# First attention layer: reciprocal rows repeated through DRAM and multiplied by GpSimd, output projection at the fourteenth head, one addition for the values' bias, three key stores

## Chip, cores and metric

One core of one Trainium2 chip runs the whole program. The metric is the device time of one execution in microseconds (us). The program is 13,733 instructions on five engines: TensorE (PE, with its weight loads as PEld), VectorE (DVE), ScalarE (ACT), GpSimd (POOL) and the SyncE queue (SP) that issues nearly all DMAs.

## What is computed

Two blocks of cross attention and mixture of experts over x of shape 16 x 128 x 256 (16 batches). Only the first attention is touched. For one batch, with 16 heads of 8 channels, T = 256 positions:

```python
q = Wq @ layernorm(x) + bq;  k = Wk @ ctx + bk;  v = Wv @ ctx + bv      # (128, T)
scores = einsum('hkt,hks->hts', q, k) / sqrt(8)
out = einsum('hts,hks->hkt', softmax(scores), v).reshape(128, T)
x = x + tanh(g_xattn[0]) * (Wo @ out + bo)
```

Then follow a sparse layer of 32 experts (routing, gathers, expert products), a second attention of 8 heads whose keys are the context itself, and a second sparse layer.

## The kernel before

The first attention is a software pipeline over steps t = -5 to 18. In step t, TensorE works through the 16 heads k of batch t (scores a second time as ST, for the exponential, and the product with the values) and through the scores S of the heads that lie 28 heads ahead, whose maxima VectorE takes. Each engine has one program, written out by hand in order, and waits on semaphores: a stalled instruction holds everything behind it on that engine. The same holds for SyncE's issues.

Per head: `scores` issues two S matmuls and two ST matmuls; there are two S banks, so the S of a head waits until VectorE has reduced the head two before it (L432). ACT exponentiates pairs of heads (L353). `values` (O, L478) runs behind heads 2, 3, 6, 7, 10, 11, 14, 15.

One PSUM bank, M1, is passed round the small products of a step; `bank()` waits until the last user's reader is done. In the order of step t: `projections` of batch t+4 behind head 1 (L503, L505), `maxima` of t+1 behind head 5 (L513), `context` (the values of t+1) behind head 9 (L494), `denominators` of t-2 behind head 12 (L520), `output` of t-2 behind head 15 (L527).

The softmax division is done late. The values' product carries a row of denominators for each head. In step b+1 SyncE copies these rows from OS into `dn` (L240) and the numerators into `on` (L243). VectorE takes `reciprocals` in step b+2 behind head 0 (L628), SyncE moves them to `rT` (16 rows, L207), TensorE spreads the rows over 128 partitions with a matmul by a 0/1 matrix (`denominators`, L520), VectorE multiplies `on` with that (`normalized`, L634, behind head 13), and TensorE multiplies by Wo (L527). ACT adds the bias and gates (`rd`, L363, first thing in step b+3, ahead of the first exponential), GpSimd adds to X (L284, first in its step b+3).

GpSimd's step t is, in order: X add (L284), the root for the layer norm (L288, waits for VectorE's statistics, taken behind head 0), the normed row (L292), four instructions that split q and k into bf16 parts (L299, L316, L319, L325), four that split the context's keys for the second attention (L269 to L275), and then `meanwhile(t)`: in step 14 the roots of the next layer's norm for rows 0 to 7 (two L788), in step 15 for rows 8 to 11 (L788).

SyncE's step t is, in order: context load (L162), the spreads of q and k parts (L174, six), the reciprocals' DMA between them (L207), dn (L240), on (L243), the shifted row (L212), a weight load or two, six key stores (L182).

VectorE adds the values' bias in two instructions behind head 10 (L669). The step's other VectorE work in steps 14 and 15 belongs to the next layer: normed rows (L1222) of rows 0 to 3 behind head 11 and of 4 to 7 behind head 15 of step 14, of 8 to 11 behind head 6 of step 15; TensorE transposes them (L833) behind heads 2, 5, 9 and 13 of step 15, each one only after the copy of the one before (L1242, behind heads 4, 6, 10, 14).

Of the kernel before, what the change touches and what calls it, by code (L numbers as in the profile page):

```python
# [15 lines left out]
P = 128  # L16
# [43 lines left out]
class Layer:  # L60


    def __init__(self, name, H, R, sem, before=None, gathers=None, keys=None, kept=None):
# [58 lines left out]


# [53 lines left out]
def keys_stored(e, w, A, M, b):  # L177

    w.wait_ge(A.keys, 4 * (b + 1))
    rows = M["keys_d"][b].rearrange("(i k) (g t) -> i g k t", k=8, g=8)  # L180
    for k in range(6):
        e.dma_start(rows[:, :, k, :], M["KW"][b % 2][:, TERMS[k][1], :]).then_inc(A.kept[b % 2], 16)  # L182


def keys_loaded(e, A, M, b):

    lo = 2048 * A.stack(b) + 1024
    e.dma_start(M["QSall"][:, lo:lo + 1024], M["keys_d"][b]).then_inc(A.ldc[b % U], 16)


def attention_sp(e, w, A, M, loads, behind_first=None):
# [4 lines left out]
    for t in A.steps():  # L196
# [7 lines left out]
        def reciprocals():  # L204
            w.wait_ge(A.rr, b5 + 1)
            w.wait_ge(A.rb, b5 - 1)
            e.dma_start(M["rT"][b5 % 2][0:H, :], M["rdn"][:, 0:2 * H]).then_inc(A.rT, 16)  # L207

# [8 lines left out]
        if within(b1):  # L217
            if not A.first and b1 >= U:

                w.wait_ge(A.st, A.NP * (b1 - U + 1))  # L220
                keys_loaded(e, A, M, b1)
            w.wait_ge(A.res2, b1 + 1)
            w.wait_ge(A.st, A.NP * (b1 - U + 1))
            for k in range(3 if b1 == 0 else 6):
                spread(e, A, M, b1, k)
                if k == 2 and within(b5) and A.first:
                    reciprocals()
            if b1 == 0 and behind_first:
                behind_first()
        elif within(b5) and not A.late(b5):  # L230
            reciprocals()
# [5 lines left out]
        if within(b4):  # L237
            w.wait_ge(A.oe, (NQ // 2) * (b4 + 1))
            w.wait_ge(A.rr, b4)
            e.dma_start(M["dn"][:, 0:2 * H], M["OS"][1:98:32, 0:NQ, :]).then_inc(A.den, 16)  # L240
            on = M["on" + A.name]
            w.wait_ge(A.pm, b4 - len(on) + 1)
            e.dma_start(on[b4 % len(on)][:, :], M["OS"][0:P:NQ, 0:NQ, :]).then_inc(A.num, 16)  # L243
        if within(b2):
# [14 lines left out]
def attention_pool(e, w, A, M, meanwhile=lambda t: None):  # L259
    H = A.H  # L260

    def keys(b):
# [4 lines left out]
        w.wait_ge(A.kept[b % 2], 96 * (b // 2))  # L267
# [9 lines left out]
    for t in A.steps():  # L277
# [135 lines left out]
def attention_pe(e, w, A, M, meanwhile=lambda t, k: None):  # L413
# [155 lines left out]
def attention_dve(e, w, A, M, meanwhile=lambda t, k: None):  # L569
# [60 lines left out]
    def normalized(b):  # L630
        on = M["on" + A.name][b % len(M["on" + A.name])]
        w.wait_ge(A.num, 16 * (A.n0 + b + 1))
        w.wait_ge(A.rb, b + 1)
# [76 lines left out]
class Routed:  # L710


    def __init__(self, sem):
# [19 lines left out]
        self.again0 = [96 * NB // 2, 96 * NB // 2, 32, 0, 0]  # L733
# [9 lines left out]
def ffn0_sp(e, w, G, A, B, M, d):  # L743
# [14 lines left out]
    def stack_ready(b):  # L758

        for k in range(2):  # L760
            w.wait_ge(B.kept[k], 96 * NB // 2)
# [1310 lines left out]
def allocate(nc, ctx, d):  # L2072
# [12 lines left out]
    for nm, shape, dt in (("VA", [P, 2, 16, 32], F32), ("QKc", [P, 2, T], F32), ("QKs", [P, 3, 2, T], BF16),  # L2085
                          ("st6", [P, 6], F32), ("mv", [P, 2], F32), ("ve", [P, 1], F32), ("rs", [P, 1], F32),
                          ("mx", [P, 2, 16], F32), ("mxT", [16, T], BF16), ("rT", [16, T], F32), ("on", [P, T], F32)):
        M[nm] = [sb(f"{nm}{n}", shape, dt) for n in range(2)]
    Cbs = sb("Cb", [P, U, T])
# [82 lines left out]
    M["keys_d"] = nc.dram_tensor("keys", [NB, P, 4 * T], F32, kind="Internal").ap()  # L2172
# [40 lines left out]
def build(nc, d, out):  # L2213
    with ExitStack() as ctx:
# [9 lines left out]
        hole, filled, gates, gamma = (sem(nm) for nm in ("hole", "filled", "gates", "gamma"))  # L2224
# [79 lines left out]
        def act_program(e):  # L2304
# [6 lines left out]
            e.activation(M["tg"][:, :], M["graw"][:, 0:4], ACT.Tanh).then_inc(gates, 1)  # L2311
# [25 lines left out]
        def dve_program(e):  # L2337
# [8 lines left out]
            def gated(t, k):  # L2346
                if t == -3 and k == 1:
                    w.wait_ge(gates, 1)
# [19 lines left out]
def orders():  # L2368
# [9 lines left out]
    return cx, cq, cv, cw  # L2378


def layout(inp):
    a = {k: np.asarray(v) for k, v in inp.items()}
    cx, cq, cv, cw = orders()
# [3 lines left out]
    for n in "qkv":  # L2387
        d["W" + n] = a["L0_xattn_W" + n][cv if n == "v" else cq][:, cx].T
# [3 lines left out]
    d["bv"] = a["L0_xattn_bv"][cv].reshape(1, 128)  # L2392
# [49 lines left out]
```

## Time and profile before

| what | value |
|---|---|
| median of 3 runs | 733.22 us (731.4 to 738.88) |
| the profiled execution | 734.11 us, span 732.3 us |
| TensorE busy | 652.4 us, 89% of the span |
| VectorE busy | 517.6 us, 71% |
| ScalarE busy | 370.8 us, 51% |
| GpSimd busy | 355.1 us, 48% |
| DMA moved | 101.12 MB, mean 138 GB/s |

The span is that of one execution's instructions; the time has about 1.8 us around it. The rows quoted below are from this execution, and their times are counted from the start of its span. The first attention lies between 19 us and 263 us.

### The profile page before, as it was taken

The numbers are of one execution on the slowest core, as the hardware profiler recorded it, in microseconds if no ns is written. First come the engines' busy times: TensorE is split into PE (matmuls) and PEld (weight loads), VectorE is DVE, ScalarE is ACT, GpSimd is POOL, SyncE is SP. The second block draws the span as 40 slices with busy tenths as digits, with TensorE's granted clock in tenths as the row PEclk, the third lists the DMA queues.
The fourth block names the chain that finished last, engine by engine and source line by source line (L and its number), as shares of the span: only waits on it lengthen the run. The fifth ranks groups of instructions, "written<-read, shape, count | busy, mean of one in ns | idle before, by whom it ended". The sixth has DMA issues, their size and how long they took to land.

```text
span 732.3 us, 13733 instructions
## 1 busy us (share of the span) xinstructions
PE 652.4 (89%) x4737; PEld 343.0 (47%) x4738; DVE 517.6 (71%) x1238; ACT 370.8 (51%) x616; POOL 355.1 (48%) x409
## 2 busy tenths in 40 slices
PE   3789999999999989989864778999989899999997
PEld 1233333333333336677541334445543367777754
DVE  3788989888889479946336898999873863333336
ACT  2147788788777634445330565666642203444430
POOL 3845646656431110077276886762010036777735
PEclk9999999999999999999995799999999999999999
DMA  6945545565633194044653667975317412222228
GB/s 149 211 108 137 147 124 140 151 177 148 171 95 88 46 308 82 6 150 139 192 166 96 190 202 194 231 208 157 109 40 235 118 33 70 87 89 88 68 95 282
DMA packets 110151, 101.12 MB, mean 138 GB/s; under 512 B 26344, under 2 KB 95629, under 8 KB 109611
## 3 DMA queue, kind: packets, MB, share of 16 engines
q1 hardware_dynamic: 100259, 80.52, 39.6%
q0 software_dynamic: 8352, 18.74, 9.1%
q10 hardware_dynamic: 1472, 0.99, 0.7%
q8 instruction: 38, 0.62, 0.4%
q14 instruction: 30, 0.25, 0.1%
HBM read 58.49 MB, written 24.40 MB: 113 GB/s over the span
## 4 chain that ended last, share of the span: by engine, by line
PE 58%; DVE 15%; issue 8%; POOL 7%; DMA 7%; SPq 3%; ACT 2%; POOLq 0%; ACTq 0%; DVEq 0%
PE O L478 12%; PE S L433 11%; PE ST L1569 6%; DVE mx L597 4%; POOL spare L305 4%; PE ST L441 3%; DMA QS<-mxT 3%; PE M L1586 2%; PE S L1586 2%; PE M L527 2%; PE M L520 2%; PE ST L1481 2%; SPq L170 1%; DMA PX<-xn,TI 1%; PE M L503 1%
## 5 line engine op out<-in xcount | busy, mean ns | idle before, releaser
L597 DVE TENSOR_REDUCE mx<-S 128x2 f32<-128x512 f32 x384 | 251.2, 684 | 37.0 <-PE S L433 35.1
L353 ACT ACTIVATE PX<-ST 128x1024 f32<-128x1024 f32 x192 | 196.1, 1023 | 95.3 <-PE ST L441 91.7
L433 PE MATMUL S<-QS 62*128 62x256 bf16 (+1 forms) x768 | 151.2, 292 | 37.0 <-DVE mx L597 29.0
L441 PE MATMUL ST<-QS 64*128 64x256 bf16 (+1 forms) x768 | 140.7, 277 | 4.5 <-DMA QS<-mxT 4.5
L478 PE MATMUL O<-PX,VA 128*32 128x256 f32 x1536 | 122.7, 392 | 0.1
L433 PEld LDWEIGHTS S<-QS 62*128 62x128 bf16 (+1 forms) x768 | 48.5, 97 | 153.9 <-DVE mx L597 98.7
L305 POOL DMA_INDIRECT spare<-ye,GI x64 | 68.2, 1066 | 26.4 <-issue 12.6
L1687 POOL DMA_INDIRECT PX<-xn,TI x39 | 39.8, 1020 | 52.6 <-DVE K1n L1881 37.2
L441 PEld LDWEIGHTS ST<-QS 64*128 64x128 bf16 (+1 forms) x768 | 53.8, 96 | 19.0 <-issue 9.0
L810 POOL DMA_INDIRECT PX<-xn,TI x32 | 34.1, 1065 | 53.6 <-DVE spare L1196 44.1
L284 POOL TENSOR_TENSOR X<-X,rd 128x256 f32<-128x256 f32 x16 | 11.6, 726 | 86.0 <-ACT rd L363 86.0
L1569 PE MATMUL ST<-EGU,Cb 128*128 x156 | 52.7, 460 | 0.3 <-ACT Cb L1642 0.3
L478 PEld LDWEIGHTS O<-PX,VA 128*32 128x32 f32 x1536 | 30.5, 108 | 41.2 <-issue 39.7
L1694 POOL DMA_INDIRECT yt<-QKc,DI x39 | 39.3, 1007 | 17.4 <-ACT QKc L1654 8.3
L288 POOL TENSOR_TENSOR rs<-ve,mhalf 128x1 f32<-128x1 f32 x32 | 18.1, 565 | 47.9 <-DVE ve L589 47.9
L316 POOL TENSOR_TENSOR QKc<-QKc,QKs 128x512 f32<-128x512 f32 (+1 forms) x29 | 27.2, 939 | 16.8 <-ACT QKs L402 15.3
L1569 PEld LDWEIGHTS ST<-EGU,Cb 128*128 128x128 f32 x156 | 26.6, 190 | 8.9 <-issue 0.6
L345 ACT ACTIVATE OS<-O 128x512 f32<-128x512 f32 x48 | 28.1, 585 | 4.2 <-PE O L478 4.2
L325 POOL TENSOR_TENSOR QKs<-QKc,QKs 128x512 bf16<-128x512 f32 (+1 forms) x29 | 27.6, 953 | 3.1 <-ACT QKs L405 1.6
L890 PE MATMUL ST<-QS,SU 128*128 128x512 f32 x64 | 28.7, 598 | 0.1
L2009 DVE TENSOR_TENSOR Xn<-ST,Xn 128x176 f32<-128x176 f32 x20 | 6.8, 342 | 30.5 <-ACT Xn L1647 30.5
L2009 DVE TENSOR_TENSOR rd<-ST,rd 128x176 f32<-128x176 f32 x19 | 6.5, 341 | 29.0 <-ACT rd L1647 29.0
(299 smaller groups left out, 1119.9 us busy)
## 6 DMA issues: line engine op xcount, KB each, us to landing
QS<-QKs SPq DMA_DIRECT2D x93, 128.0 KB
QS<-keys SPq DMA_DIRECT2D x16, 512.0 KB, 5.5
keys<-spare SPq DMA_DIRECT2D x96, 64.0 KB, 2.3
QS<-QKs SPq DMA_DIRECT2D x93, 64.0 KB
EGU<-in_ew SPq DMA_DIRECT2D x16, 256.0 KB, 4.4
xn<-spare SPq DMA_DIRECT2D x8, 512.0 KB, 10.9
ye<-QKc SPq DMA_DIRECT2D x32, 128.0 KB, 2.1
VA<-in_val SPq DMA_DIRECT2D x16, 256.0 KB, 3.7
```

The costliest lines, as they stand in the source:

```text
L305: e.indirect_dma_start(out=M["GA"][b7 % 3][:, T * k:T * k + T], out_offset=None, in_=M["ye_d"], in_offset=bass.IndirectOffsetOnAxis(ap=M[" ...
L353: e.activation(M["PX"][pair % 4][:, :], M["ST"][pair % 2][:, :], ACT.Exp, scale=A.scale).then_inc(A.exp, 1)
L433: got = e.matmul(M["S"][n % 2][:, 256 * a:256 * a + 256], QS[:, 0, 128 * a:128 * a + 128], QS[:, 1, :], start=True, stop=True)
L441: got = e.matmul(M["ST"][(NP * t + k // 2) % 2][:, 512 * u + 256 * a:512 * u + 256 * a + 256], QS[:, 1, 128 * a:128 * a + 128], QS[:, 0, : ...
L478: got = e.matmul(M["O"][32 * u:32 * u + 32, 256 * (quad % 2):256 * (quad % 2) + 256], V[:, a, 4 * quad + u, :], M["PX"][pair % 4][:, 512 * ...
L597: e.tensor_reduce(M["mx"][b % 2][:, :, A.row_of_max(head)], M["S"][n % 2][:, :].rearrange("p (a s) -> p a s", a=2), AX.X, ALU.max, negate= ...
L810: e.indirect_dma_start(out=M["GX"][x % GATHERS], out_offset=None, in_=M["xn_d"], in_offset=bass.IndirectOffsetOnAxis(ap=M["TI"][:, x:x + 1 ...
L890: got = e.matmul(M["BK"][3 + n % 2], M["SU"][:, a, 128 * c:128 * c + 128], M["XT0"][:, a, 512 * g:512 * g + 512], start=(a == 0), stop=(a ...
L1569: got = e.matmul(BK[3 + 2 * (j % 2)][:, 0:2 * I1], M["XeT1"][j % 2][:, 128 * a:128 * a + 128], M["EGU"][:, bass.ds(expert[j], 1), a, :], s ...
L1586: got = e.matmul(BK[1 if j % 2 else 7][:, 0:T], M["HT1"][j % 2][0:HALF, 128 * a:128 * a + 128], M["ED"][:, bass.ds(expert[j], 1), a, :], s ...
L1687: e.indirect_dma_start(out=M["XE1"][i % TILES], out_offset=None, in_=M["xn1_d"], in_offset=bass.IndirectOffsetOnAxis(ap=M["TI1"][:, i:i + ...
L1694: e.indirect_dma_start(out=M["yt_d"], out_offset=bass.IndirectOffsetOnAxis(ap=M["DI1"][:, j:j + 1], axis=0), in_=M["YE"][j % 4][:, :], in_ ...
```

## The change

For batches 0 to 13 of the first attention (`by_rows`):

- the reciprocals are taken one step earlier, behind head 8 of step b+1; SyncE writes them to DRAM (`den_d`, 4 rows of 1024), and in the next step copies that to `row_d` with each row repeated 8 times (DRAM to DRAM, 128 KB), and loads `row_d` into RB, 128 x 256, behind the `on` copy and ahead of the shifted row;
- GpSimd multiplies `on` with RB behind its four key instructions and ahead of `meanwhile`; the matmul L520 and VectorE's product L634 are gone;
- `output` comes behind head 13 and not 15.

Batches 14 and 15 keep the old way. Besides, for all batches: the bias of the values is added in one instruction of 128 x 256 (Wv's columns and bv reordered on input), the six key stores become three of 3, 2 and 1 terms with the DRAM tensor laid out by term, and the gates' semaphore is folded into another.

```diff
+    def by_rows(self, b):
+        return self.first and 0 <= b < NB - 2
...
-    rows = M["keys_d"][b].rearrange("(i k) (g t) -> i g k t", k=8, g=8)
-    for k in range(6):
-        e.dma_start(rows[:, :, k, :], M["KW"][b % 2][:, TERMS[k][1], :]).then_inc(A.kept[b % 2], 16)
+    rows = M["keys_d"][b].rearrange("k i (g t) -> (i g) k t", g=8)
+    for j, lo, hi in ((0, 0, 3), (1, 3, 5), (2, 5, 6)):
+        part = M["KW"][b % 2][:, j, :].unsqueeze(1).to_broadcast([P, hi - lo, T // 2])
+        e.dma_start(rows[:, lo:hi, :], part).then_inc(A.kept[b % 2], 16)
...
+        def repeated():
+            w.wait_ge(A.rT, 16 * (b5 + 1))
+            w.wait_ge(A.rows, 32 * (b5 - 1))
+            e.dma_start(M["row_d"][b5 % 2].rearrange("(j i) x -> j i x", j=4),
+                        M["den_d"][b5 % 2].unsqueeze(1).to_broadcast([4, A.R, NQ * T])).then_inc(A.rows, 16)
...
-                if k == 2 and within(b5) and A.first:
-                    reciprocals()
+                if k == 2 and A.by_rows(b5):
+                    repeated()
...
+        elif A.by_rows(b5):
+            repeated()
...
+        if A.by_rows(b5):
+            w.wait_ge(A.rows, 32 * b5 + 16)
+            w.wait_ge(A.on, b5 - 1)
+            e.dma_start(M["RB"][b5 % 2][:, :], M["row_d"][b5 % 2].rearrange("r (g t) -> (r g) t", g=NQ)).then_inc(A.rows, 16)
...
+        if A.by_rows(b4):
+            w.wait_ge(A.rr, b4 + 1)
+            e.dma_start(M["den_d"][b4 % 2], M["rdn"][:, 0:2 * H]).then_inc(A.rT, 16)
         if A.first and within(t + 1):
             keys_stored(e, w, A, M, t + 1)
...
+        b5 = t - 2
+        if A.by_rows(b5):
+            on = M["on" + A.name][b5 % 2]
+            w.wait_ge(A.rows, 32 * (b5 + 1))
+            w.wait_ge(A.num, 16 * (b5 + 1))
+            e.tensor_tensor(on[:, :], on[:, :], M["RB"][b5 % 2][:, :], ALU.mult).then_inc(A.on, 1)
         meanwhile(t)
...
-                if k == 12 and within(b5):
+                if k == 12 and within(b5) and not A.by_rows(b5):
                     denominators(b5)
-                if k == 15 and within(b5):
+                if k == (13 if A.by_rows(b5) else 15) and within(b5):
                     output(b5)
...
-                if k == 0 and within(b5):
+                if k == 0 and within(b5) and not A.by_rows(b5):
                     reciprocals(b5)
+                if k == 8 and A.by_rows(t - 1):
+                    reciprocals(t - 1)
...
-                    for a in range(2):
-                        v = lambda ap: ap.rearrange("p (c r g) -> p c g r", c=4, g=NQ)
-                        o = M["VA"][b2 % 2][:, a, 0:H, 0:32:NQ].rearrange("p (g c) r -> p c g r", c=4)
-                        got = e.tensor_tensor(o, v(M1[:, 128 * a:128 * a + 128]), v(M["bv"][:, :]), ALU.add)
-                    got.then_inc(A.va, 1)
-                if k == 13 and within(b5):
+                    bv = M["bv"][:, :].rearrange("p (h r) -> p h r", r=A.R).unsqueeze(1).to_broadcast([P, 2, H, A.R])
+                    e.tensor_tensor(M["VA"][b2 % 2][:, :, :, 0:32:NQ],
+                                    M1[:, 0:256].rearrange("p (a h r) -> p a h r", a=2, r=A.R), bv, ALU.add).then_inc(A.va, 1)
+                if k == 13 and within(b5) and not A.by_rows(b5):
                     normalized(b5)
```

## Rows read from the trace of the kernel before

**Rows 1.** Steps 1, 7, 12: length; PE, PEld, DVE, ACT, POOL busy; clock; DMA share, GB/s.
```profile
56.19:69.06 12.87, 12.09 (x142) 4.32 (x138) 11.52 (x22) 10.05 (x14) 7.35 (x10) 1.00 0.53 139
135.63:148.93 13.30, 12.93 (x144) 5.09 (x143) 11.91 (x23) 10.69 (x14) 8.07 (x11) 1.00 0.63 173
202.30:214.93 12.63, 11.88 (x141) 4.41 (x142) 11.30 (x20) 9.85 (x12) 2.80 (x5) 1.00 0.51 130
```

**Rows 2.** Chain that ended last, in order of time (start, us, what): end of step 7.
```profile
145.67 0.62 PE M L520 x2
...
148.37 0.64 PE M L527 x2
149.04 0.57 ACT rd L363
149.74 0.67 PE M L503 x2
```

**Rows 3.** Timeline of VectorE, step 7 and the start of 8: start, us, instruction.
```profile
142.66 1.94 DVE L597 TENSOR_REDUCE mx<-S 128x2 f32<-128x512 f32 x3 [0.20 <-PE S L433]
144.52 0.68 DVE L669 TENSOR_TENSOR VA<-M,bv 128x128 f32<-128x128 f32 x2
145.11 1.29 DVE L597 TENSOR_REDUCE mx<-S 128x2 f32<-128x512 f32 x2
...
147.26 0.41 DVE L634 TENSOR_TENSOR on<-M,on 128x256 f32<-128x256 f32 x1
...
150.71 0.35 DVE L628 RECIPROCAL rdn<-dn 128x32 f32<-128x32 f32 x1
150.98 1.82 DVE L597 TENSOR_REDUCE mx<-S 128x2 f32<-128x512 f32 x3
```

**Rows 4.** Timeline of ACT: the last exponential of step 7.
```profile
147.87 1.02 ACT L353 ACTIVATE PX<-ST 128x1024 f32<-128x1024 f32 x1 [0.15 <-PE ST L441]
```

**Rows 5.** Timeline of GpSimd, step 7 and the start of 8.
```profile
137.57 0.56 POOL L288 TENSOR_TENSOR rs<-ve,mhalf 128x1 f32<-128x1 f32 x1 [0.47 <-DVE ve L589]
...
144.80 0.67 POOL L275 TENSOR_TENSOR spare<-spare 128x256 bf16<-128x256 f32 x1
149.68 0.72 POOL L284 TENSOR_TENSOR X<-X,rd 128x256 f32<-128x256 f32 x1 [4.20 <-ACT rd L363]
```

**Rows 6.** Timeline of SyncE's issues, step 7.
```profile
140.38 0.60 SPq L240 DMA_DIRECT2D dn<-OS  x1
141.36 0.59 SPq L243 DMA_DIRECT2D on<-OS  x1
...
143.71 3.81 SPq L182 DMA_DIRECT2D keys<-spare  x6
```

**Rows 7.** DMA issues: size, median us from issue to landing.
```profile
EGU<-in_ew SPq DMA_DIRECT2D x16, 256.0 KB, 4.4
...
Cb<-in_ctx SPq DMA_DIRECT2D x15, 128.0 KB, 2.4
```

**Rows 8.** Timeline around the reciprocals' DMA of batch 14: SyncE, then TensorE.
```profile
250.08 0.59 SPq L207 DMA_DIRECT2D rT<-rdn  x1
252.40 0.29 PEld L520 LDWEIGHTS M<-rT,hbL 16*128 16x128 f32 x2 [0.41 <-DMA rT<-rdn]
```

**Rows 9.** Timeline of GpSimd in steps 14 and 15: the next layer's roots.
```profile
233.27 1.03 POOL L788 TENSOR_TENSOR frs<-fve,mhalf 128x4 f32<-128x4 f32 x1 [4.31 <-DVE fve L1217]
...
240.85 1.02 POOL L788 TENSOR_TENSOR frs<-fve,mhalf 128x4 f32<-128x4 f32 x1 [0.21 <-DVE fve L1217]
```

**Rows 10.** Timeline of SyncE in step 15: the numerators' copy.
```profile
243.49 0.58 SPq L243 DMA_DIRECT2D on<-OS  x1
```

**Rows 11.** Timeline of VectorE, steps 15 and 16.
```profile
243.38 1.37 DVE L1222 TENSOR_SCALAR spare<-X,fmv,frs 128x256 f32<-128x256 f32 x4
...
249.71 0.34 DVE L628 RECIPROCAL rdn<-dn 128x32 f32<-128x32 f32 x1
```

**Rows 12.** Timeline of TensorE, step 15: the fourth transposition.
```profile
248.41 0.66 PE L833 MATMUL S<-ident,spare 128*128 128x128 f32 x4
```

More of the change, by code:

```diff
@@ L96, in __init__ @@
             self.kp, self.yb = one("kp"), one("yb")
+            self.rows = one("rows")
             self.vt, self.va = one("vt"), one("va")
@@ L205, in reciprocals @@
             w.wait_ge(A.rr, b5 + 1)
-            w.wait_ge(A.rb, b5 - 1)
+            if A.first:
+                w.wait_ge(A.on, b5 - 1)
+            else:
+                w.wait_ge(A.rb, b5 - 1)
             e.dma_start(M["rT"][b5 % 2][0:H, :], M["rdn"][:, 0:2 * H]).then_inc(A.rT, 16)
+        def repeated():
[3 more added lines that the diff above has]
+                        M["den_d"][b5 % 2].unsqueeze(1).to_broadcast([4, A.R, NQ * T])).then_inc(A.rows, 16)
         def shift_rows():
@@ L265, in keys @@
         w.wait_ge(A.ldc[b % U], 16 * (b // U + 1))
-        w.wait_ge(A.kept[b % 2], 96 * (b // 2))
+        w.wait_ge(A.kept[b % 2], 48 * (b // 2))
         w.wait_ge(A.keys, 4 * b)
@@ L518, in denominators @@
         w.wait_ge(A.rT, 16 * (A.n0 + b + 1))
+        if A.first:
+            w.wait_ge(A.on, b)
         bank()
@@ L632, in normalized @@
         w.wait_ge(A.num, 16 * (A.n0 + b + 1))
-        w.wait_ge(A.rb, b + 1)
+        w.wait_ge(A.rb, b + 1 - (NB - 2 if A.first else 0))
         e.tensor_tensor(on[:, :], M1[:, 256:512], on[:, :], ALU.mult).then_inc(A.on, 1)
@@ L732, in __init__ @@
         self.again = [one(f"again{u}") for u in range(E0 - PLACES)]
-        self.again0 = [96 * NB // 2, 96 * NB // 2, 32, 0, 0]
+        self.again0 = [48 * NB // 2, 48 * NB // 2, 32, 0, 0]
         self.at = {}
@@ L751, in ffn0_sp @@
     for k in (6, 7):
-        e.dma_start(M["keys_d"].rearrange("b (i k) x -> k (b i) x", k=8)[k],
-                    d["hole"][:, 3072:4096].to_broadcast([NB * P // 8, 1024])).then_inc(B.kept[2], 16)
+        e.dma_start(M["keys_d"][:, k, :, :],
+                    d["hole"][:, 3072:4096].unsqueeze(1).to_broadcast([NB, P // 8, 1024])).then_inc(B.kept[2], 16)
     w.wait_ge(G.dve, G.at["wd"])
@@ L760, in stack_ready @@
         for k in range(2):
-            w.wait_ge(B.kept[k], 96 * NB // 2)
+            w.wait_ge(B.kept[k], 48 * NB // 2)
         w.wait_ge(B.kept[2], 32)
@@ L2086, in allocate @@
                           ("st6", [P, 6], F32), ("mv", [P, 2], F32), ("ve", [P, 1], F32), ("rs", [P, 1], F32),
-                          ("mx", [P, 2, 16], F32), ("mxT", [16, T], BF16), ("rT", [16, T], F32), ("on", [P, T], F32)):
+                          ("mx", [P, 2, 16], F32), ("mxT", [16, T], BF16), ("RB", [P, T], F32), ("on", [P, T], F32)):
         M[nm] = [sb(f"{nm}{n}", shape, dt) for n in range(2)]
+    M["rT"] = [m[0:16, :] for m in M["RB"]]
     Cbs = sb("Cb", [P, U, T])
@@ L2171, in allocate @@
     M["ye_d"] = nc.dram_tensor("ye", [E0 * CAP + P, T], F32, kind="Internal").ap()
-    M["keys_d"] = nc.dram_tensor("keys", [NB, P, 4 * T], F32, kind="Internal").ap()
+    M["keys_d"] = nc.dram_tensor("keys", [NB, 8, P // 8, 4 * T], F32, kind="Internal").ap()
+    for nm, rows in (("den", 4), ("row", 32)):
+        two = nc.dram_tensor(nm, [2, rows, 4 * T], F32, kind="Internal").ap()
+        M[nm + "_d"] = [two[n] for n in range(2)]
     M["ew_d"] = d["ew"]
@@ L2223, in build @@
         M["n_e"] = 16 * (EARLY + 3)
-        hole, filled, gates, gamma = (sem(nm) for nm in ("hole", "filled", "gates", "gamma"))
+        hole, filled, gamma = (sem(nm) for nm in ("hole", "filled", "gamma"))
         M["hole"], M["gamma"] = hole, gamma
@@ L2310, in act_program @@
             w.wait_ge(M["w_g"], 16)
-            e.activation(M["tg"][:, :], M["graw"][:, 0:4], ACT.Tanh).then_inc(gates, 1)
+            w.wait_ge(filled, 1)
+            e.activation(M["tg"][:, :], M["graw"][:, 0:4], ACT.Tanh).then_inc(filled, 1)
             attention_act(e, w, L0, M, ffn0_act_meanwhile(e, w, X, L0, M))
@@ L2347, in gated @@
                 if t == -3 and k == 1:
-                    w.wait_ge(gates, 1)
+                    w.wait_ge(filled, 2)
                     e.tensor_tensor(M["tg"][:, 2:3], M["tg"][:, 2:3], M["graw"][:, 4:5], ALU.mult).then_inc(gamma, 1)
@@ L2377, in orders @@
     cw = 16 * (2 * (p // 32) + p % 2) + p % 32 // 2
-    return cx, cq, cv, cw
+    ch = 8 * head(p // 8, 4) + p % 8
+    return cx, cq, cv, cw, ch
 def layout(inp):
     a = {k: np.asarray(v) for k, v in inp.items()}
-    cx, cq, cv, cw = orders()
+    cx, cq, cv, cw, ch = orders()
     d = {"x": a["x"][:, cx, :], "ctx": a["ctx_2048"][:, cx, :]}
@@ L2387, in layout @@
     for n in "qkv":
-        d["W" + n] = a["L0_xattn_W" + n][cv if n == "v" else cq][:, cx].T
+        d["W" + n] = a["L0_xattn_W" + n][ch if n == "v" else cq][:, cx].T
     d["Wo"] = a["L0_xattn_Wo"][cx][:, cv].T
@@ L2391, in layout @@
         d["b" + n] = a["L0_xattn_b" + n][cq].reshape(128, 1)
-    d["bv"] = a["L0_xattn_bv"][cv].reshape(1, 128)
+    d["bv"] = a["L0_xattn_bv"][ch].reshape(1, 128)
     d["perm"] = np.equal(cw[:, None], cx[None, :]).astype(np.float32)
```

3 lines of the change are left out of this document (2 added, 1 removed).

## Prediction

> **What bounds the kernel now.** I read the busy shares by step first, then the chain that ended last, then the timelines of one step. Inside the first attention the steps repeat within a few hundredths of a microsecond, so one step (7) stands for steps 3 to 11. It lasts 13.30 us, with TensorE busy 12.93 of them, VectorE 11.91, ACT 10.69, GpSimd 8.07 [rows 1]. TensorE looks like the plain bound, and the change takes a matmul pair of 0.62 us out of each of 14 steps [rows 2]: 8.7 us, were it all on the path. But step 1, which has neither the denominators nor the output product (0.62 + 0.64 us less), still lasts 12.87 us: 1.26 us less of TensorE's work bought 0.43 us, with its idle time up from 0.37 to 0.78 [rows 1]. That is the warning. TensorE and VectorE run in lockstep through two S banks, and at the end of a step the chain hops from TensorE to ACT's `rd` and back to L503, which needs the bank M1 [rows 2]. What counts is where in the step the work is taken out, and where it is put back.
>
> **One step, walked through.** All times are step 7's.
>
> *Behind head 12.* L520 runs from 145.60 to 146.22. Head 13's scores need the maximum of head 11 done. It starts at 145.11 and takes 0.65 (1.29 for two), with 0.09 or so until TensorE resumes: 145.85 [rows 3]. So L520 mostly fills a wait. Without it TensorE gets on 0.37 us earlier, not 0.62.
>
> *VectorE ahead of that.* The two bias additions last from 144.52 to the next maximum at 145.11, 0.59 us; one instruction of 128 x 256 should cost what L634 does, 0.41 with some 0.08 overlapped, 0.33. That saves 0.26. The reciprocals, moved behind head 8, cost 0.27 there (150.71 to 150.98), in the stretch in which three maxima run back to back from 142.66 [rows 3]. They cancel: maximum 11 starts when it did. VectorE loses L634 (0.33), where nobody waits for it in the new order, and the reciprocals of the step's start. Bounds for the new addition: 0.33, and 0.59 if its four-dimensional pattern brings no gain.
>
> *The output product.* It keeps its 0.63 us but stands behind head 13, ahead of heads 14 and 15. So head 15's scores are issued 0.63 - 0.37 + 0.05 (one more change between small groups and matmuls) = 0.31 us later than now.
>
> *The step's end.* Now head 15's exponential starts at 147.87 [rows 4]; the next ACT work can follow 0.92 behind it, at 148.79, but `rd` starts at 149.04 because L527 ends at 149.01 [rows 2]. In the new order L527 is long over, and ACT is the limit: 147.87 + 0.31 + 0.92 = 149.10. L503 follows `rd` by 0.70 as now. It comes at 149.80 and not 149.74. So steps 3 to 11 **gain nothing**: +0.06 us each, +0.6 with step 2. Bounds: from -0.43 (step 1's length, [rows 1]) to +0.3 (if the new addition brings nothing, 0.26 more behind head 11), nine or ten times: -4 to +3 us. I take the walk's value, which uses the rows of the very step.
>
> *GpSimd's product.* From the root at 137.57 GpSimd works without a gap to 145.47 [rows 5]. The product follows; L284, of the same shape with two SBUF inputs, takes 0.72, so with signals `on` is ready at 146.3. In the new order the root no longer waits for VectorE's statistics much (they come 0.4 us earlier, and the X add sets it), and counted from L503 `on` is ready 0.2 to 0.3 us before TensorE has finished head 13's scores. Cost 0, with little cover: a product longer by 0.3 us lengthens each step one for one. The Trainium skill (GPSIMD Engine Reference, Engine selection) says the reverse of this change: elementwise work with two inputs belongs on VectorE, GpSimd being about twice as slow. Here it is 0.72 against 0.41, and by this rule the product left on VectorE would have `on` 0.3 us sooner; by the walk nobody would use that.
>
> *The DMAs.* dn is issued at 140.38, behind ACT's copy; a DMA of the same 16 KB took 2.3 us from issue to TensorE's start (250.08 to 252.40, [rows 8]), so it lands at 142.7, and VectorE reaches the reciprocals at 143.3 [rows 3, 6]. 0.6 us of cover; if it is gone, VectorE stalls with all maxima behind it. The copy to 8-fold rows is issued one step later, some 5 us ahead of the RB load. That load goes out behind `on`, at about 142.0, and must land by 145.47. 128 KB out of DRAM took 2.4 us [rows 7]: 144.4, cover 1.1 us. Behind the RB load on SyncE wait the shifted row (needed only in the next step) and the loads. No row shows a DRAM to DRAM copy. The fit in the Trainium skill (DMA: Bandwidth & Descriptors, Anatomy of one DMA) would give 2.3 us for 128 KB as an estimate; I only need it under 5, and 256 KB took 4.4 [rows 7].
>
> *Key stores.* Six issues in 3.81 us [rows 6], 0.64 each, become three: 1.9 us less, 0.6 back for `den_d`, on a queue that nobody waits for in these steps. At the start of step 2 a context load behind such stores is on the chain once; what it hides is close behind. I take -0.1 (bounds -1.3 and 0). Loading these keys in the second attention moves the same 4 KB rows: 0.
>
> **Steps 12 to 14 start.** There are no projections here, so no hop over `rd`. Behind head 15, TensorE goes straight to head 0 and to head 2, which needs head 0's maximum: L527's 0.63 us are saved whole. The same step then pays 0.31 behind head 13. Three starts saved and three payments (steps 11 to 13): 3 x (0.31 - 0.63) = -1.0. Bounds 0 and -1.9.
>
> **The tail, steps 14 to 16.** Here GpSimd's product stands ahead of `meanwhile`, and `meanwhile` holds roots for which VectorE waits, and then TensorE. In step 15 the RB load can go out only behind `on`, now at 243.49 [rows 10], in the new order some 0.7 earlier (step 14 is shorter by L520), RB at 243.4, landed at 245.8, product to 246.6, root (1.02, [rows 9]) to 247.7. That root now starts at 240.85. VectorE's four normed rows, now at 243.38 [rows 11], start at 247.7 and end at 249.0; the copy queued behind them ends at 249.7, and only then may TensorE transpose the fourth pair, now at 248.41 [rows 12]. TensorE resumes at 249.8, 1.3 us later than now, though it had 1.2 us less to do. In step 14 the same happens to the first two roots (now 233.27, then 236.0), with VectorE 0.8 us late. The late step end then delays the old-way reciprocals of batch 14 (249.71, [rows 11]) to about 251.1, and their DMA, 2.3 us [rows 8], TensorE's L520 in step 16 from 252.4 to 253.5. **+1.1 us**, in place of the 1.2 gained by two matmul pairs. Bounds -1.2 and +3.
>
> **Sum.** -0.1 + 0.6 - 1.0 + 1.1 = +0.6 us on the profiled execution's 734.11. That execution lies 0.9 above the median of 733.22, so for a median: 733.9.
>
> **Rivals.** (1) *TensorE's share is real everywhere.* Each step gains the whole 0.62 because the lockstep slackens (VectorE also has 0.33 less per step), and the roots are not late. For: TensorE 97% busy. Against: step 1. Price 14 x 0.62 = 8.7: 724.5; with the tail as above, 727.
>
> (2) *RB comes late* (the slower side). It shares the rings with the `on` copy and a weight load. It decides from 3.5 us of landing time on. At 4.4, as 256 KB took [rows 7], the product starts at 146.4, `on` is ready 1.0 us after it would be, 0.7 of it beyond the cover, in some 13 steps: +9, 743; at 3.9, +3. The measured 2.4 speaks against it.
>
> (3) *The tail is dearer*: dn or RB land 1 us later in steps 14 and 15 and roots, norms and transposes follow, 2 to 4 us: 736 to 738.
>
> (4) *The change doesn't do what it says*: the broadcast DMAs, with three or eight times the pieces, cost SyncE more than 0.6 us each, so that context loads and spreads come late: some 2 us, 736.
>
> **How the numbers follow.** Forecast (nothing wins or loses over 3 us): 0.62, its own range 731 to 737. (1) 0.14, (2) 0.08, (3) 0.11, (4) 0.05. Runs that 1% (7.3 us) separates are about what a measurement of this kernel can tell apart. Faster by over 1% needs nearly all of (1): 0.09. Slower by over 1% needs (2) at its worst: 0.07. Within 1%: 0.84. The range takes in (3) and (4), half of (1) and half of (2), and leaves out some 1 in 10: 727 to 739.
>
> **What would show it.** Right: steps 3 to 11 last 13.2 to 13.5 us with TensorE's idle time doubled to 0.8 or more; head 13's scores wait for a maximum; L503 waits for `rd`, and `rd` for the exponential, not for L527; GpSimd's idle time before the X add shrinks to some 3.5 us; L1222 waits for L788, and L788 comes behind the product in steps 14 and 15. Wrong: steps of 12.9 us or less (rival 1); GpSimd idle ahead of the product, with the RB load as releaser, in steps 3 to 11 (rival 2); VectorE idle ahead of the reciprocals. The shakiest terms are the step's end, where 0.3 us of ACT decide nine times over, and the tail.

## The result and the profile after

After: 741.28 us median (737.62 to 745.56, 14 runs), beside 733.81 (730.15 to 738.88, 14 runs) for the kernel before on the same chip. Ratio 1.0107 [1.0083, 1.0131]: 7.5 us slower, where 0.7 was forecast and 739 was the range's end. The profiled execution took 741.61 us, span 739.8 (before 734.11 and 732.3), so the two profiles show nearly the whole difference. In two later groups of runs every kernel, the one before too, took 25 to 28 us longer, so absolute times are compared only within a group. GpSimd's X addition marks every step from step 3 on; it sorts the difference:

| stretch | before | after | difference |
|---|---|---|---|
| start of the span to first X addition | 82.83 | 82.96 | +0.1 |
| first to thirteenth (steps 3 to 14) | 157.08 | 156.83 | -0.3 |
| thirteenth to sixteenth (steps 15 to 17) | 23.26 | 28.52 | +5.3 |
| sixteenth to the end of the span | 469.1 | 471.5 | +2.4 |

Steps 3 to 11 came out as forecast. 5.3 us lie in the last steps, and 2.4 behind them, where only the DRAM layout of the keys differs. These are two single executions; how far such a stretch varies is shown below.

*The body.* Busy time by windows, columns as in [rows 1]: step 7 and step 12.
```profile
135.68:149.05 13.37, 12.46 (x144) 4.70 (x142) 11.67 (x21) 10.47 (x15) 8.78 (x12) 1.00 0.66 191
202.60:215.38 12.78, 11.49 (x140) 4.03 (x136) 10.99 (x19) 9.64 (x13) 3.53 (x6) 1.00 0.57 159
```
Step 7 lasts 13.37 us against 13.30: TensorE's idle time rose from 0.37 to 0.91, so most of what was taken out became idle time. The chain at the step's end, which answers [rows 2]:
```profile
148.17 0.61 PE O L512 x8
...
149.16 0.57 ACT rd L397
...
149.87 0.67 PE M L537 x2
```
The output product no longer stands between the last exponential and `rd`; it is on the chain earlier, at 146.32 for 0.63 us. ACT's timeline names the limit: `rd` follows the exponential by 0.92 us, and L537 (L503 before) follows `rd` by 0.71.
```profile
148.24 1.03 ACT L387 ACTIVATE PX<-ST 128x1024 f32<-128x1024 f32 x1 [0.83 <-PE ST L475]
149.16 0.56 ACT L397 ACTIVATE rd<-M,bog,tg 128x256 f32<-128x256 f32 x1
```
VectorE in the same step, answering [rows 3]; the distance between two starts is what an instruction costs the queue:
```profile
143.32 0.34 DVE L664 RECIPROCAL rdn<-dn 128x32 f32<-128x32 f32 x1
143.58 1.22 DVE L633 TENSOR_REDUCE mx<-S 128x2 f32<-128x512 f32 x2
144.72 0.67 DVE L705 TENSOR_TENSOR VA<-M,bv 128x256 f32<-128x256 f32 x1
145.21 1.86 DVE L633 TENSOR_REDUCE mx<-S 128x2 f32<-128x512 f32 x3
```
The reciprocals cost 0.26 here. The single bias addition costs 0.49 from start to start, against 0.59 for the two before; the chain, which counts from end to end, gives it 0.58. GpSimd, answering [rows 5], has no idle time ahead of the product, `on<-on,RB`:
```profile
145.12 0.73 POOL L363 TENSOR_TENSOR on<-on,RB 128x256 f32<-128x256 f32 x1
149.80 0.72 POOL L311 TENSOR_TENSOR X<-X,rd 128x256 f32<-128x256 f32 x1 [3.94 <-ACT rd L397]
```

*Step 12.* Here, and in steps 2 and 14, VectorE does wait for dn ahead of the reciprocals:
```profile
209.57 0.35 DVE L664 RECIPROCAL rdn<-dn 128x32 f32<-128x32 f32 x1 [0.37 <-DMA dn<-OS]
```
The chain reaches it through SyncE's issues of the spreads; dn is issued at 206.59 and takes 2.95 us.

*Step 15.* GpSimd, VectorE and TensorE there (answering [rows 9, 11, 12]), each from its own timeline:
```profile
246.22 0.73 POOL L363 TENSOR_TENSOR on<-on,RB 128x256 f32<-128x256 f32 x1 [5.70 <-DMA RB<-row]
246.91 1.02 POOL L824 TENSOR_TENSOR frs<-fve,mhalf 128x4 f32<-128x4 f32 x1
```
```profile
247.96 1.38 DVE L1258 TENSOR_SCALAR spare<-X,fmv,frs 128x256 f32<-128x256 f32 x4 [4.57 <-POOL frs L824]
249.26 0.68 DVE L1278 COPY QS<-S 128x512 f32<-128x512 f32 x1
```
```profile
247.40 0.70 PE L563 MATMUL M<-on,Wo 128*128 128x256 f32 x2
250.00 0.76 PE L869 MATMUL S<-ident,spare 128*128 128x128 f32 x4 [1.90 <-DVE QS L1278]
```
The late root was walked to within 0.4 us (forecast: root ends 247.7, norms end 249.0, copy 249.7, TensorE 249.8; here 247.93, 249.34, 249.94, 250.00). What came behind it was not forecast. Windows of the changed kernel, columns as before; the last but two is TensorE's granted clock:
```profile
248.00:250.00 2.00, 0.10 (x2) 0.01 (x1) 1.94 (x5) 1.04 (x2) 0.00 (x0) 1.00 0.00 0
250.00:252.00 2.00, 2.00 (x14) 0.74 (x14) 0.95 (x2) 0.00 (x0) 0.00 (x0) 0.60 0.03 8
252.00:260.00 8.00, 7.90 (x36) 1.96 (x32) 0.42 (x1) 2.08 (x3) 0.73 (x1) 0.50 0.19 47
```
and of the kernel before:
```profile
248.00:250.00 2.00, 2.00 (x18) 0.91 (x18) 1.33 (x3) 1.22 (x2) 0.00 (x0) 1.00 0.00 0
250.00:260.00 10.00, 9.34 (x57) 3.67 (x55) 2.78 (x6) 4.41 (x6) 1.45 (x2) 1.00 0.38 108
```
After 1.9 us of idle time the granted clock fell to 0.50, the 1.2 GHz level, and it stayed there till past 260. TensorE was busy nearly throughout, but its matmuls took longer: the 24 of L512 from 252.77 on took 3.12 us, where eight take 0.64 at full clock.

### The profile page after: what moved, and what is told of

Read it like the earlier page. It is cut to its first block, busy times and chain, and to the rows that moved or that the text cites. A ratio compares the mean times of both kernels' runs of the same rounds, so it can differ in the third digit from the quotient of the medians.

```text
span 739.8 us, 13643 instructions
## 1 busy us (share of the span) xinstructions
PE 649.4 (88%) x4710; PEld 337.7 (46%) x4710; DVE 511.8 (69%) x1208; ACT 368.1 (50%) x616; POOL 363.5 (49%) x423
## 4 chain that ended last, share of the span: by engine, by line
PE 48%; DVE 19%; issue 10%; DMA 9%; POOL 7%; SPq 3%; ACT 2%; ACTq 0%; POOLq 0%; DVEq 0%
PE S L467 9%; PE O L512 9%; DVE mx L633 6%; PE ST L1605 6%; POOL spare L332 4%; DMA QS<-mxT 3%; PE ST L475 2%; PE M L1622 2%; PE S L1622 2%; PE M L563 2%; DMA PX<-xn,TI 2%; PE ST L1517 2%; PE M L537 1%; POOL PX L846 1%; DVE PX L1219 1%
## 5 line engine op out<-in xcount | busy, mean ns | idle before, releaser
L387 ACT ACTIVATE PX<-ST 128x1024 f32<-128x1024 f32 x192 | 196.3, 1024 | 103.0 <-PE ST L475 98.3
L467 PE MATMUL S<-QS 62*128 62x256 bf16 (+1 forms) x768 | 154.1, 293 | 42.0 <-DVE mx L633 32.2
L475 PE MATMUL ST<-QS 64*128 64x256 bf16 (+1 forms) x768 | 143.9, 279 | 5.6 <-DMA QS<-mxT 5.3
L512 PE MATMUL O<-PX,VA 128*32 128x256 f32 x1536 | 125.0, 399 | 0.2
L512 PEld LDWEIGHTS O<-PX,VA 128*32 128x32 f32 x1536 | 30.8, 109 | 42.9 <-issue 41.2
L537 PE MATMUL M<-Xn,Wq 128*128 128x256 f32 x32 | 13.5, 509 | 16.5 <-ACT tg L2352 7.0
```

The lines of the kernel that those rows point to most:

```text
L387: e.activation(M["PX"][pair % 4][:, :], M["ST"][pair % 2][:, :], ACT.Exp, scale=A.scale).then_inc(A.exp, 1)
L467: got = e.matmul(M["S"][n % 2][:, 256 * a:256 * a + 256], QS[:, 0, 128 * a:128 * a + 128], QS[:, 1, :], start=True, stop=True)
L475: got = e.matmul(M["ST"][(NP * t + k // 2) % 2][:, 512 * u + 256 * a:512 * u + 256 * a + 256], QS[:, 1, 128 * a:128 * a + 128], QS[:, 0, : ...
L512: got = e.matmul(M["O"][32 * u:32 * u + 32, 256 * (quad % 2):256 * (quad % 2) + 256], V[:, a, 4 * quad + u, :], M["PX"][pair % 4][:, 512 * ...
```

## The experiments

Ratios are to the kernel before, run beside the others on the same chip. The two slower groups are i, n and p (before: 760.72 us) and x, y and z (758.95). Windows and X times come from one profiled execution of each kernel. "First to last X" is the time between the first and the sixteenth X addition, 180.34 us before and 185.35 after.

### The last steps

**a_roots_first**: in step 15 alone, GpSimd's roots stand ahead of the product.
```diff
+        if t == NB - 1:
+            meanwhile(t)
         b5 = t - 2
...
-        meanwhile(t)
+        if t != NB - 1:
+            meanwhile(t)
```


> The change with one swap: in step 15 GpSimd takes the next layer's root (L788 of before) ahead of its product. Theory (tail and clock): in the changed kernel TensorE stands idle for 1.9 us at 248.1 because the root waits behind the product, and the granted clock then is 0.50 from 250.8 to 260.5; with the root at about 242.3 neither happens, the step 15 to 17 part takes back 4 to 5 us, and the time is 736 to 737. Rival (the tail's loss comes from elsewhere, the late DMA of the rows or a clock that falls anyway): no change, 741. Rival (the loss is in the steps themselves): no change either, with the clock at 1.00.


735.26 us, 1.0043 [1.0020, 1.0066], span 732.0. First to last X 180.03. GpSimd's root is back at its place, and the product still has its RB row to wait for:
```profile
240.91 1.02 POOL L827 TENSOR_TENSOR frs<-fve,mhalf 128x4 f32<-128x4 f32 x1 [0.82 <-DVE fve L1256]
245.90 0.73 POOL L365 TENSOR_TENSOR on<-on,RB 128x256 f32<-128x256 f32 x1 [3.97 <-DMA RB<-row]
```
TensorE is busy 1.88 of 2.00 us from 248 to 250 and the clock stays at 1.00 till 260. First to last X is 5.3 us shorter than in the changed kernel: the last steps' loss comes from the order of root and product.

**b_rows_to_12**: the old way from batch 12 on (`b < NB - 4` in place of `NB - 2`).


> The change for batches 0 to 11 only, 12 to 15 the old way, so that no product by GpSimd stands in steps 14 and 15. Theory (tail and clock): X of the last batch comes as early as before (263 us), time 736. If instead steps 2 to 13 were what costs, it stays at 740 or more.


736.48 us, 1.0046 [1.0023, 1.0069]; thirteenth to sixteenth X addition 22.74, clock 1.00. The same loss vanishes another way. (First to last X is 181.2, with two steps of 13.8 and 14.35 us in this execution.)

**c_filler**: six unneeded 128 x 128 matmuls where TensorE waits for the fourth transposition; their results are overwritten.
```diff
+                if h == 3:
+                    for _ in range(6):
+                        e.matmul(BK[1][:, 0:128], M["ident"][:, :], M["Wo"][:, :], start=True, stop=True)
```


> The change with six spare matmuls (128x128, into an unused bank) that TensorE does in step 15 behind head 13, where it would wait for the late copy. The stall stays (the root is as late), only TensorE is busy in it. Theory (the half clock follows from TensorE's idle time): granted clock 1.00 up to 258 us, 3.5 to 4 us back, 737 to 738. Rival (the stall alone costs and the clock is a chance thing): 741, or later by what the fillers take.


737.7 us, 1.0089 [1.0054, 1.0124]. The stall is left, the clock is not lost:
```profile
248.00:250.00 2.00, 1.22 (x12) 1.04 (x10) 1.91 (x5) 0.79 (x1) 0.00 (x0) 1.00 0.00 0
250.00:260.00 10.00, 9.22 (x60) 3.37 (x60) 2.99 (x6) 3.92 (x5) 1.45 (x2) 1.00 0.20 57
```
Thirteenth to sixteenth X addition: 23.26 before, 24.65 here, 28.52 after. So in these executions 1.4 us are the walked delay and 3.9 the clock. As a time, 1.0089 cannot be told from 1.0107: the clock's share rests on the traces, and it varies (last section).

### The body

**d_out15**: the output stays behind head 15.
```diff
-                if k == (13 if A.by_rows(b5) else 15) and within(b5):
+                if k == 15 and within(b5):
```


> The change with the output product behind head 15 again, not 13; all else as changed. Theory (the walk through a step: the 0.63 us put ahead of heads 14 and 15 push the last exponential, rd and L503 back): steps 3 to 11 last 12.9 to 13.0 us in place of 13.37, 3 to 4 us back in all, and the tail as bad as changed: 737 to 738. Rival (GpSimd's chain or VectorE sets the step): steps stay at 13.3 to 13.4, 741.


738.92 us, 1.0102 [1.0070, 1.0134]. Steps last 13.26 us, 0.11 less, not 12.9 to 13.0: the theory missed, the rival's range is missed by 0.04.

**e_roots_out15**: a and d together.


> Both repairs: in step 15 the root ahead of GpSimd's product, and the output product behind head 15. In the runs before, the first gave back 4 to 5 us of the tail and left 3 us over the kernel before; the second shortened steps 3 to 11 from 13.37 to 13.26 only. If the two add up, 1 us below the first: ratio to the kernel before 1.003. If the 3 us that are left sit in the steps, it falls to 1.000.


734.27 us, 1.0030 [1.0005, 1.0055]; steps 13.25. The two moves add up, as expected.

**h_late_reciprocals**: e with the reciprocals behind head 14 and their store behind the next context load.
```diff
-                if k == 8 and A.by_rows(t - 1):
+                if k == 14 and A.by_rows(t - 1):
```


> Both repairs, and the reciprocals behind head 14 and not 8 (their DMA to DRAM goes behind the next context load). In the run with the output behind head 15 the chain ran through VectorE behind heads 8 to 13: reciprocals 0.34, bias addition 0.58, maxima without a gap. Theory (the reciprocals' 0.27 us at that place are on the path, the price that the walk set against the bias addition's saving): steps 3 to 11 at 13.0, 2 to 3 us below the run without it. Rival (they only fill a wait for TensorE): steps at 13.26.


734.05 us, 1.0008 [0.9986, 1.0031]; steps 13.24, as the rival said. The wait for dn in step 12 is gone. VectorE holds the step here: three maxima and the bias addition stand back to back, and head 13's scores wait for the maximum behind them.
```profile
127.63 1.94 DVE L635 TENSOR_REDUCE mx<-S 128x2 f32<-128x512 f32 x3 [0.20 <-PE S L469]
129.49 0.65 DVE L707 TENSOR_TENSOR VA<-M,bv 128x256 f32<-128x256 f32 x1
129.94 2.62 DVE L635 TENSOR_REDUCE mx<-S 128x2 f32<-128x512 f32 x4
```
```profile
130.67 0.70 DVE mx L635
...
131.42 0.28 PE S L469
```
(The second fence is the chain.) With TensorE's matmul gone and the output and the reciprocals at the best places that were tried, the change gains 0.06 us of a step's 13.30.

### SyncE and the keys

**g_roots_old_keys**: a, with the six stores and the layout of before.


> The change with the root ahead of the product in step 15 and with the six key stores of before. Theory (keys' layout): the 3 us that the first repair left over are gone, ratio 1.000 to 1.001, loads of keys at 5.5. Rival (what is left over sits elsewhere): 1.004 as with the first repair alone.


741.9 us, 1.0121 [1.0088, 1.0154]. Most steps last 13.8 to 14.4 us, one 15.95. The expected 1.000 was missed. The chain now runs through SyncE's six stores (L187), which hold back the context load:
```profile
137.22 0.57 SPq L187
...
141.45 2.11 DMA Cb<-in_ctx
143.61 0.70 PE M L541 x2
```
So the queue has no room for the three added DMAs beside six stores. Yet from the sixteenth X addition to the end it took 467.3 us, the least of all; before 469.1, and nine profiles with the new layout unpadded 469.5 to 474.5, mean 471.5.

**f_keys_only** and, on another chip, **r_keys_same_chip**: the kernel before with the three stores and their layout alone.
```diff
-    rows = M["keys_d"][b].rearrange("(i k) (g t) -> i g k t", k=8, g=8)
-    for k in range(6):
-        e.dma_start(rows[:, :, k, :], M["KW"][b % 2][:, TERMS[k][1], :]).then_inc(A.kept[b % 2], 16)
+    rows = M["keys_d"][b].rearrange("k i (g t) -> (i g) k t", g=8)
+    for j, lo, hi in ((0, 0, 3), (1, 3, 5), (2, 5, 6)):
+        part = M["KW"][b % 2][:, j, :].unsqueeze(1).to_broadcast([P, hi - lo, T // 2])
+        e.dma_start(rows[:, lo:hi, :], part).then_inc(A.kept[b % 2], 16)
```


> The kernel before with the three key stores and the DRAM tensor by term, and nothing else of the change. Theory (the keys' new layout costs in the second attention: the loads of 512 KB took a median 6.3 us to land in the changed kernel and 5.5 before): slower by 2 to 3 us, ratio 1.003 to 1.004, with loads at 6.0 or more. Rival (the extra DMA traffic or chance): 1.000, loads at 5.5.

> The kernel before with the three key stores and their layout alone, once more, beside the padded one on one chip. Theory (the stores' layout costs the second half): 1.003 to 1.008. Rival (the first ratio of 1.0055 was spread between executions): 0.998 to 1.002.


736.66 us, 1.0055 [1.0033, 1.0077], and 736.26 us, 1.0052 [1.0022, 1.0081]. Steps unchanged at 13.30. The edit that was priced at nothing behind the first attention costs some 4 us. f lies above the 1.003 to 1.004 expected of it, r inside its 1.003 to 1.008.

**i_six_stores_layout**: the layout with six stores.
```diff
+    for k in range(6):
+        e.dma_start(rows[:, k, :], M["KW"][b % 2][:, TERMS[k][1], :]).then_inc(A.kept[b % 2], 16)
```


> The kernel before with the keys' tensor in DRAM laid out as in the changed kernel (terms, then rows), but written by six stores of 64 KB as before, so that only the addresses change. Theory (the layout makes the 512 KB loads of the keys in the second attention land later, and these cost the second half some 4 us): ratio 1.003 to 1.008, as with three stores, keys' loads landing at 5.8 us or more against 5.5. Rival (the number of stores matters, or the 0.5% of the run with the keys alone was chance): 0.998 to 1.002. Steps of 13.30 us in either case.


763.48 us beside 760.72, 1.0027 [1.0006, 1.0047]. So the layout seems to cost without the three stores too, but the interval only just leaves out no change.

**n_rows_padded** and **s_padded_same_chip** (beside r): f with 17 rows for each term (`[NB, 8, P // 8 + 1, 4 * T]`). **v_after_padded**: the same in the changed kernel. **p_h_padded** and **w_late_padded_same_chip**: in h.


> The kernel before with three key stores and the changed kernel's layout, but with 17 rows for each term in DRAM instead of 16, so that the eight rows that neighbouring partitions read no longer lie 64 KB apart but 68 KB. Theory A (rows at a power-of-two distance meet in the same part of DRAM): ratio 0.998 to 1.002, loads back at 5.5 us. Theory B (scattered rows of 4 KB are dearer than one run of 512 KB, whatever the distance): 1.003 to 1.008, as with three stores alone. Rival (0.5% was chance): about 1.000, and the six-store kernel too.

> The same with 17 rows for each term instead of 16. Theory A (rows 64 KB apart meet): 0.998 to 1.002 and at least 0.003 under the unpadded one of this call. Theory B (scattered rows): the same as the unpadded one within 0.002.

> The changed kernel with 17 rows for each term and nothing else altered. Theory A: what is left is the last steps of the first attention, 5.1 us, so 1.005 to 1.008. Theory B: 1.009 to 1.012 as the changed kernel. First to last X addition 185.3 us in both.

> The changed kernel with the context's copies of step 15 ahead of the product, the output behind the fifteenth head, the reciprocals behind the fourteenth and their store after the next context's load, as in the last run of this kind (1.0008), and 17 rows for each term. Theory A: the second half gives its 3 to 4 us back, ratio 0.994 to 0.998, so faster than both kernels. Theory B: 1.000 to 1.002. First X addition to last 179 us in both.

> The version with the context's copies of step 15 first, output behind head 15, late reciprocals and 17 rows, once more, to see whether it beats the kernel before: theory A 0.996 to 1.000, its steps of 13.24 us and its shorter last steps giving 1.1 us between first and last X addition; theory B 1.000 to 1.002.


n 1.0006 [0.9983, 1.0028]; s 1.0039 [1.0015, 1.0063], beside r's 1.0052; v 1.0107 [1.0067, 1.0147], as without padding; p 0.9994 [0.9969, 1.0020] and w 1.0002 [0.9978, 1.0026], against h's 1.0008. n against f is for the distance; s, v, p and w, each against its unpadded kernel, see nothing. Nor do the keys' loads land sooner: their median is 6.2 us in s, 6.0 in v and 5.9 in w, against 5.6 to 6.3 in nine unpadded profiles. Padding is not shown to help. The Trainium skill (DMA: Bandwidth & Descriptors, Latency and other measured facts) gives 207 GB/s for copies at a row pitch of 512 KiB, 164 at 2 MiB and 103 at 4 MiB, and the full rate again at 4 MiB with 4 KiB of padding; 64 KB is below all these pitches, and no run here shows such a mending.

**x_behind_keys, y_behind_before, z_behind_late**: in f, before and h, the second attention's load of the keys is issued at the end of its step.
```diff
-            if not A.first and b1 >= U:
-
-                w.wait_ge(A.st, A.NP * (b1 - U + 1))
-                keys_loaded(e, A, M, b1)
...
+        if not A.first and within(b1) and b1 >= U:
+            w.wait_ge(A.st, A.NP * (b1 - U + 1))
+            keys_loaded(e, A, M, b1)
```


> The kernel before with the three key stores and their layout, and in the second attention each load of the keys (512 KB) issued at the end of its step instead of ahead of the six spreads and the row of maxima. Theory (the chain of the second attention runs through SyncE's keys load, 0.44 us to issue before and 0.58 with the layout, through the spreads and through the landing of the 4 KB row of maxima, 4.4 to 5.4 us, which is late because 512 KB go ahead of it): the row's landing falls to 2 to 4 us and the layout's price leaves the chain, so at least 4 us under the unmoved one (1.0055, 1.0052): 0.985 to 1.000. Rival (the layout's price lies elsewhere, in the stores or behind the attention): 1.003 to 1.008.

> The kernel before with the same move of the keys' loads and nothing else. Theory: 0.984 to 0.998, and equal to the moved one with the new layout within 0.002, since neither the issue nor the landing of these loads is on the chain any longer. Rival: 0.998 to 1.002, with the new layout's 0.5% staying between the two.

> The changed kernel with the copies of step 15 first, the output behind head 15, the late reciprocals (1.0008 and 1.0002 so far) and the same move of the keys' loads. Theory: under both moved ones by the 1.1 us between first and last X addition, 0.983 to 0.997, the fastest version of this study. Rival: 0.999 to 1.002.


x 826.73 us, 1.0894 [1.0857, 1.0930]; y 815.81, 1.0753 [1.0718, 1.0789]; z 828.05, 1.0909 [1.0869, 1.0948]. A plain miss: I had taken the keys to be wanted three steps later, and the chain shows scores waiting for them in eleven of twelve steps. But now these loads are bare on the chain. The last five in y (old layout) took 4.20, 4.01, 4.61, 4.42 and 3.65 us, in x (new layout) 6.28, 5.43, 5.43, 5.13 and 4.86. First and last of them, from the chain of y:
```profile
534.15 4.20 DMA QS<-keys
...
579.11 3.65 DMA QS<-keys
```
and of x:
```profile
536.28 6.28 DMA QS<-keys
...
590.10 4.86 DMA QS<-keys
```
In these five the same 512 KB land 1.2 us later out of rows 64 KB apart (means 5.43 and 4.18). In the seven loads before them, of which six stand on each chain, there is no difference in the mean (5.88 in x, 5.80 in y), so the layout does not cost at every load; what sets the five apart is not known. x is 10.9 us above y, more than the landings: behind the longer wait TensorE's matmuls are slower in x. The eight of L478 behind the first of the five loads, on the chain of x, and of L477, on that of y:
```profile
543.47 1.01 PE O L478 x8
```
```profile
539.03 0.57 PE O L477 x8
```
From the first to the last of these loads y takes 44.96 us and x 53.82; the landings are 5.0 of these 8.9 us. In the unmoved kernels the load's issue at SyncE (minimum, median, maximum in ns) went from
```profile
L188 SPq DMA_DIRECT2D QS<-keys x16: 319/443/580, 351.4 to 511.8; - x16
```
to, in the changed kernel,
```profile
L194 SPq DMA_DIRECT2D QS<-keys x16: 545/576/1044, 355.6 to 518.7; - x16
```
and the median landing from 5.5 to 6.3 us (5.0 in g, old layout; 5.6 to 6.3 in the nine profiles with the new one). Behind that load in the queue stand the spreads and the row of maxima, for which the scores wait. The chain of before, two pieces of one step:
```profile
453.56 0.49 SPq L188
...
457.96 4.86 DMA QS<-mxT
```
and of r:
```profile
460.07 0.58 SPq L189
...
464.59 5.67 DMA QS<-mxT
```
This step is not typical. The row's landings on the chain between 410 and 530 us are no longer with the new layout: before 5.44, 4.86, 4.02 and 4.36, mean 4.67; r 4.99, 5.67 and 4.71, mean 5.12; f 4.20 and after 4.53 in the mean of five each. Nor do the steady steps hold most of the loss. From the sixteenth X addition to the issue of the fifth row of maxima (439.00 before), before and g take 175.8 and 175.6 us, the nine profiles with the new layout 177.2 to 180.4, mean 178.0. From there to the end it is 293.3 and 291.7 against 292.2 to 295.7, mean 293.5. So in the mean 2.3 of 3.3 us arise by the second attention's first steps; its first four key loads stand in that stretch.

## Why the prediction was wrong

**Steps 3 to 11: right, in part by luck.** 13.36 us forecast, 13.37 measured, by the walked chain: `rd` behind the exponential, L537 behind `rd`, TensorE's idle time past 0.8. Rival 1 falls, and in these steps rival 4 too: SyncE issues the three stores in some 1.5 us together, the copy to 8-fold rows in 0.67 and RB's load in 0.53 (medians). But two terms on VectorE were off and cancelled. The bias addition costs 0.49 to 0.59, not 0.33, near its upper bound. The reciprocals were charged with 0.27, and yet the bias addition starts only 0.15 us later in its step than before (9.04 us behind the step's start, against 8.89), because the maxima around them close up. The output's new place, charged with 0.31 us, is worth 0.11 (d); with it put back, VectorE holds the step at 13.24 (h).

**GpSimd's product and RB: right; dn only in steps 3 to 11.** 0.73 measured for 0.72, and no wait for RB or dn in steps 3 to 11. The product waits for RB in steps 12 to 15. The 0.6 us of cover for dn fail in step 2 (1.07 us of idle time) and in steps 12 and 14 (0.37 each). The RB load waited for the copy to 8-fold rows in two of 14 steps, 0.9 us in all. The fit in the Trainium skill that was quoted for it (DMA: Bandwidth & Descriptors, Anatomy of one DMA) is stated for DMAs that GpSimd issues, and SyncE issues this one; no run here shows its landing. The Trainium skill's rule that such work belongs on VectorE (GPSIMD Engine Reference, Engine selection) decided nothing in these steps, and in step 15 it was not the product's length but its wait, with the root queued behind it, that cost time.

**Steps 12 to 14: -1.0 forecast.** The thirteenth X addition less the tenth: 36.92 before, 36.52 after, so -0.4, inside the bounds. But a, c and v, the same program in these steps but for v's padding, took 37.41, 37.05 and 36.97, so the mean of the four is +0.1: the forecast gain was mostly not there. Steps 13 and 14 do gain some 0.3 each. Step 12, 12.62 before, takes 12.79 after and 13.28 to 13.58 in the other three, where the wait for dn is 0.86 to 1.16:
```profile
209.04 0.35 DVE L667 RECIPROCAL rdn<-dn 128x32 f32<-128x32 f32 x1 [1.16 <-DMA dn<-OS]
```
This row is from a. The term that failed here is dn's cover, carried over from step 7. h, with late reciprocals, has no such wait and takes 12.57.

**The tail: the largest term that failed, +1.1 forecast, +5.3 measured, bound +3.** The mechanism was right to TensorE's restart at 250.00. The sum went on from there at full clock. I had foreseen an idle stretch of more than a microsecond and did not ask what it does to the clock. In the trace TensorE was idle 1.9 us and then had 0.50 for 9 us; with filler matmuls 1.00, at a price of 1.4 us for the whole tail instead of 5.3. The Trainium skill (TensorE: Matmul & The Clock Gate, What's actually happening) has the two levels and ties them to how busy the engine has been lately, and the trace agrees that an idle stretch can bring the lower one. By that page this tail could have a second term, and it was a rival I left out. Rival 3 named the place, with another mechanism and too small a price.

**Key stores: "the same 4 KB rows: 0" failed.** Measured +0.5% with nothing else changed (f, r), +2.4 us in the two profiles. Same rows and bytes, but the order in DRAM counts. That the three stores with their layout cost is shown (f, r). That the layout alone does rests on i, at the edge of its interval, and on the loads: issue 0.13 us longer, median landing 5.6 to 6.3 us against 5.0 and 5.5, and 1.2 us more in five bare ones (x, y). How this becomes 4 us in the unmoved kernels stays open: most of it arises before the steady steps, and the row of maxima lands no later. And "a queue that nobody waits for in these steps" holds only with the three stores: with six (g) the chain runs through it, 1.0121. Three stores into the old layout were not tried, nor another issuing queue for the load.

**No version beat the kernel before**: the best, h, with its padded form, gave 1.0008, 0.9994 and 1.0002. The parts do not quite add up: h has the new layout, which costs 4 us in f and r, and gains 1.4 us between first and last X, so it should stand near 1.0035. The mean of the three is 1.0001, and where the other 2.5 us went no trace shows.

**The sum.** It was 733.8 by its own terms, not 733.9, which changes nothing. In the two profiles the tail is 4.2 us over its term and the stretch behind the first attention 2.4 over; together they are 6.6 of the 6.9 us between 0.6 and 7.5. That dn's wait was small in this execution is luck.

## What to carry to other kernels

Removing matmuls from an engine that is 97% busy is worth what the next chain leaves: walk the step again, and expect idle time in their place. Walk the first and last steps apart from a typical one: a DMA's cover in the middle (dn) need not hold there. If the walk ends in an idle TensorE of one or two microseconds (1.9 here), price the clock behind it too, and never queue an engine's small, urgent operation (the root) behind one that waits for a DMA. A store made cheaper by another DRAM layout may be paid for by whoever loads it: price the load's issue and landing, and look up who waits for it before moving it.

## What the hardware showed unexpectedly

The same stall costs a different time in each execution. In v, step 15 is the same up to the stall, and the clock recovers after some 4 us:
```profile
250.00:252.00 2.00, 1.94 (x16) 0.82 (x16) 0.95 (x3) 0.00 (x0) 0.00 (x0) 0.86 0.03 8
252.00:254.00 2.00, 1.90 (x17) 0.60 (x20) 0.00 (x0) 1.48 (x2) 0.24 (x1) 0.50 0.05 8
254.00:256.00 2.00, 2.00 (x15) 0.63 (x8) 0.16 (x1) 0.60 (x1) 0.48 (x1) 0.78 0.00 0
```
Thirteenth to sixteenth X addition: 25.52 us there, 28.52 in the changed kernel's profile. In d, idle for 2.52 us there, the clock is 0.50 from 252 to 254 and 1.00 again from 256. The stall's price is therefore 2.3 to 5.3 us by execution; a's 1.0043 against 1.0107, 4.7 us and uncertain by 2.4, estimates its mean. The Trainium skill (TensorE: Matmul & The Clock Gate, What's actually happening) calls the number of slow matmuls at a kernel's start variable from run to run; here the same holds for a slow stretch in the middle. Also, a VectorE addition of 128 x 256 out of PSUM with the values' strided output takes 0.67 us, against 0.41 for L634's plain product; and GpSimd's product was not lengthened by VectorE's work beside it (0.73 against 0.72).
